# A ring of three pairs of PSUM banks, divided by use

## The reference, cut to what matters

```python
x = x + _layernorm(_L0_ffn_ref(_layernorm(x), ...))
# _L0_ffn_ref: D = 128, H = 16 heads of 8, E = 8 experts, K = 2, FF = 512
q = (x @ Wq + bq); k = (x @ Wk + bk); v = (x @ Wv + bv)      # by head; q, k rotated
attn = softmax(einsum('bhqd,bhkd->bhqk', q, k) / sqrt(HD))   # 1024 x 1024 per head
x1 = layernorm(x + (attn @ v) @ Wo + bo)
# two best of eight experts per token, weighted
h = gelu(einsum('bsd,edf->bsef', x1, W1) + b1); y = einsum('bsef,efd->bsed', h, W2) + b2
return layernorm(x1 + sum_e comb_e * y_e)
```

## Time and profile before

| | |
|---|---|
| median of 2 runs | 2870.24 us (2866.96 to 2873.52) |
| the profiled execution | 2869.59 us, span 2867.9 us |
| VectorE busy | 2243.4 us, 78% |
| ScalarE busy | 1236.5 us, 43% |
| TensorE busy | 1195.6 us, 42% |
| GpSimd busy | 289.9 us, 10% |
| mean granted clock of TensorE | 0.94 |

### The profile page before, as it was taken

The page is one execution under the profiler, slowest core; times in us unless marked ns, Lnnn a source line. Parts: engine busy times, 40 slices in busy tenths (PEclk is TensorE's granted clock), DMA queues, the critical chain, the costliest instruction groups (busy, mean ns, idle before and its releaser), DMA issues. The chain is left out here.

```text
span 2867.9 us, 37860 instructions
## 1 busy us (share of the span) xinstructions
PE 1195.6 (42%) x7272; PEld 536.4 (19%) x7272; DVE 2243.4 (78%) x15187; ACT 1236.5 (43%) x3176; POOL 289.9 (10%) x425
## 2 busy tenths in 40 slices
PE   3010100101010000101004887788876887778697
PEld 1000000000000000000001111223421342133365
DVE  5999999999999999999975899856657665864133
ACT  1333333333333333333360556656655664567542
POOL 0000000000000000000010020031023212201211
PEclk9999999999999999999996899979987998889898
DMA  5000000000000000000034020103110212001100
GB/s 135 1 1 1 1 1 1 1 1 1 1 1 1 1 1 1 1 1 1 1 68 103 1 67 20 24 22 89 26 44 23 74 37 52 18 17 30 33 1 23
DMA packets 79603, 66.11 MB, mean 23 GB/s; under 512 B 8126, under 2 KB 64232, under 8 KB 79368
## 3 DMA queue, kind: packets, MB, share of 16 engines
q1 hardware_dynamic: 76296, 57.40, 8.3%
q0 software_dynamic: 3072, 6.30, 0.7%
HBM read 34.77 MB, written 28.57 MB: 22 GB/s over the span
## 5 line engine op out<-in xcount | busy, mean ns | idle before, releaser
L1309 DVE TENSOR_REDUCE nm_half<-pair 128x2 f32<-128x1024 f32 x512 | 611.7, 1219 | 224.1 <-PE pair L1557 188.6
L203 ACT ACTIVATE ex<-row,nmax 128x65 f32<-128x65 f32 x960 | 336.0, 350 | 923.8 <-DVE nmax L305 837.3
L1196 ACT ACTIVATE pt<-pair 128x1024 f32<-128x1024 f32 x512 | 510.2, 1027 | 389.2 <-PE pair L1567 357.9
L263 DVE SCALAR_TENSOR_TENSOR junk<-ex,tab 128x65 f32<-128x65 f32 x2850 | 620.0, 218 | 1.4 <-issue 0.4
L366 PE MATMUL p_s<-tab,bdg 128*128 128x32 f32 x120 | 31.9, 406 | 829.2 <-DVE tab L268 829.2
L1533 PE MATMUL p_o<-pt,va 128*9 128x512 f32 x2048 | 299.2, 659 | 9.7 <-ACT pt L1196 8.3
L268 DVE TENSOR_TENSOR tab<-raw,rz 128x1 f32<-128x1 f32 (+1 forms) x1890 | 284.8, 151 | 3.2 <-issue 1.1
L297 DVE SCALAR_TENSOR_TENSOR junk<-ex,rz,row 128x65 f32<-128x65 f32 x930 | 265.4, 285 | 3.0 <-issue 2.7
L1557 PE MATMUL pair<-ks,qs 48*128 48x512 bf16 x1024 | 212.8, 420 | 123.3 <-ACT pt L1196 75.4
L1567 PE MATMUL pair<-qs,ks 50*128 50x512 bf16 x1024 | 209.7, 414 | 62.4 <-DVE nm_half L1309 30.4
L263 DVE DVE_READ_ACCUMULATOR junk<-ex,tab 128x1 f32 x2850 | 233.8, 82 | 0.3
(11 more groups left out here) (254 smaller groups left out, 1908.1 us busy)
## 6 DMA issues: line engine op xcount, KB each, us to landing
parts_dram<-parts SPq DMA_DIRECT2D x48, 256.0 KB, 3.6
qs<-parts_dram SPq DMA_DIRECT2D x32, 192.0 KB, 4.8
ks<-parts_dram SPq DMA_DIRECT2D x32, 192.0 KB, 5.4
hid<-xs_dram SPq DMA_DIRECT2D x15, 256.0 KB, 2.9
ys_dram<-hid SPq DMA_DIRECT2D x15, 256.0 KB, 2.4
h_dram<-f SPq DMA_DIRECT2D x20, 128.0 KB, 2.5
x<-in_x SPq DMA_DIRECT2D x4, 512.0 KB, 8.4
w_W<-in_W SPq DMA_DIRECT2D x1, 2048.0 KB
```

The lines of the kernel that those rows point to most:

```text
L203: nc.scalar.activation(ex[:, r % 2, :], row[:, r % 2, 1:], ACT.Exp, bias=nmax[:, r % 2:r % 2 + 1], accum_out=z[:, r % 2:r % 2 + 1]).then_i ...
L263: nc.vector.scalar_tensor_tensor(junk[:, g, :], ex[:, k, :], 1.0, tab[:, g, r:r + ROW], ALU.mult, ALU.mult, accum_out=raw[:, g:g + 1]).the ...
L1196: nc.scalar.activation(pt[:, kt % 2, :, tokens(t)], pair[fill.pair][:, :, :], ACT.Exp, scale=SCALE).then_inc(s_exp, 1)
L1309: nc.vector.reduce_max(nm_half[:, t, hp % 2, :, q], pair[fill.pair][:, :, :], AX.X, negate=True)\
```

## The change

Two lists of uses take the place of one. Maxima (A) always use `pair[2]`, and an A waits for the maximum of the A before it. B, HS and HH alternate between `pair[0]` and `pair[1]`, and each waits for the evacuation of the use two before it of these three kinds. The list of steps, the tensors and the instructions are the same; only the pair and the value waited for differ.

```diff
--- before.py
+++ after.py
@@ -836,18 +836,20 @@
 
 
 
-    pairs = []
+    scores, maxima = [], []
 
     def one(steps, s, ring, n):
         for x in steps:
-            prior = pairs[-PAIRS] if len(pairs) >= PAIRS else None
-            fill = Fill(ring, n, len(pairs) % PAIRS, prior)
+            used = maxima if x[0] == "A" else scores
+            first, count = (2, 1) if x[0] == "A" else (0, 2)
+            prior = used[-count] if len(used) >= count else None
+            fill = Fill(ring, n, first + len(used) % count, prior)
             if x[0] == "T":
                 steps_of(x[1:], s - 1, fill)
             else:
                 steps_of(x, s, fill)
             if x[0] in ("A", "B", "HS", "HH"):
-                pairs.append((x[0], pair_index(x, s)))
+                used.append((x[0], pair_index(x, s)))
             n += bank_uses(x)
         return n
```

## The result

The changed kernel takes 3083.28 us (3080.42 to 3086.14, 2 runs) against 2870.24: a ratio of 1.0735, interval 1.0695 to 1.0775. It is slower, as forecast, but by 213 us where 131 were forecast, and 3 us beyond the range.

What follows compares the result with a forecast made beforehand. VectorE was taken to bound batch 0 (205 of 225 us), no engine being full in batches 1 to 3. Terms 12 + 81 + 38 = 131 us on 2870 gave 3000 us, 4.5% slower, range 2930 to 3080.

Steps and rivals of the forecast that it cites:

- Unit cost: Back-to-back maxima: with one pair, fill and evacuation alternate, 1.71 us apart instead of 1.13, or 1.93 at 1.2 GHz.
- the sum of 1.53: Between maxima at 2.4 GHz: A, PV, B and the next A start within 1.53 us, fitting into 1.71.
- Prologue, +12: Opening run of 16 maxima: 15 distances grow from 1.13 to 1.93 us, +12 us, hidden by nothing.
- Batch 0, +81: Batch 0: 160 maxima alternating with their fills, +68 us, plus some time at the lower clock, +13 us.
- I allow 8 of the 64 steps: Batch 0: 8 more loop steps at the lower clock, 1.67 us extra each, +13 us.
- my middle of 68: Batch 0: alternation alone costs +68 us, between +49 (other work and idle time absorbed) and +88 (neither absorbed).
- rival (a): Clock falls through batch 0: all 64 steps slow, 107 us in place of 13, 3094 us in all; chance 0.16.
- Batches 1 to 3, +38: Batches 1 to 3: +24 for eight stretches, +32 for bunched maxima, -18 for vanished exponential waits; between -20 and +75 us.
- the gain of 18 us from exponentials: Batches 1 to 3: a quarter of TensorE's 75.4 us idle before As on exponentials goes, -18 us.
- The 56 bunched ones: Batches 1 to 3: 56 maxima starting less than 1.3 us behind the one before lose 0.58 us each, +32 us.
- The eight stretches: Batches 1 to 3: eight stretches between expert groups, 11 maxima each, grow from 126.1 to 150.5 us, +24.
- Costed at nothing: Two pairs for exponentials and expert products, and the routed products' 21.5 us of idle time put down to maxima: 0 us.

Runs made afterwards that it cites:

- Filling the gaps: Changed kernel with matmuls whose result nobody reads added in batch 0, in 78 gaps between two maxima tiles holding at most one B: 3051.21 us, ratio 1.0599.
- the other order: Changed kernel with the second of two maxima tiles in batch 0 issued behind the value product PV, not directly behind the first: 3067.67 us, ratio 1.0672.
- the opposite division: Changed kernel with the split reversed, two pairs for maxima and one shared by exponentials and expert products: 2970.92 us, ratio 1.0348.

## Why the prediction was wrong

The direction and the alternation held; two terms of the sum failed: the time at the lower clock in batch 0, put far too low, and a gain in batches 1 to 3 that did not come.

*Unit cost.* 1.71 and 1.93 us: the prologue shows 1.93 to the hundredth. In batch 0 maxima with no other VectorE work between them start 1.71 to 1.73 us apart at 2.4 GHz, with PV and B in the gap as well, as the sum of 1.53 had it; at 1.2 GHz 1.93 is the usual distance with PV or B alone in the gap, and 2.79 with both. Right.

*Prologue, +12.* 12. Right.

*Batch 0, +81.* 119. The step that failed is "I allow 8 of the 64 steps" at the lower clock, +13. The clock was low for 205 of 345 us, 182 more than before, which is some 31 steps of 5.95 us. At the price I had worked out (1.67 us for such a step) that is 51 us, and 68 + 51 = 119; that it comes out to the us is luck. Filling the gaps took 152 us of low clock away and gave 36 us, which is a price of 0.24 for one us at the lower level where I had 0.28. By this estimate the clock costs some 43 us, at least, since the added matmuls are in the 36, and the alternation at most 76, within its bounds and a little above my middle of 68. I had the argument in hand, 0.66 busy against 0.80, and put it into rival (a) as all or nothing, 64 steps or 8; it came out half way, and I gave (a) 0.16.

The Trainium skill, "TensorE: Matmul & The Clock Gate", section "A second HAM failure mode: psum-queue depth-cycling", describes a kernel that cycles through PSUM banks, where small idle gaps make the clock swing between its levels. The trace agrees on the swing, with 18 spells at the lower level in batch 0; that the gaps cause it is not shown here, as the other order left one of them empty and the clock as it was.

*Batches 1 to 3, +38.* 86, or 83 with the change in them alone (68 in its profiled execution, at the clock of before). The second step that failed is the gain of 18 us from exponentials. It was judged by one stall, in which the maximum happened to be early. In these batches TensorE waited 73 us for exponentials before As; now it waits 134 us for maxima, and exponentials are no longer among the main releasers there. The distances between maxima, sorted as the prediction had them, say the same. The 56 bunched ones lost 34 us in the changed kernel and 31 in the run with the change in these batches alone, against +32: right. The eight stretches lost 30 and 22, against +24. The other 199, which the gain should have made 18 us shorter, became 19 and 11 us longer. Why they did is open; part of the 19 goes with the clock, which lay low for 80 us more than before and only 7 more in the other run. The +24 rested on a misreading: the bounds of the earlier trace rows cut maxima at both ends, so a distance there was 1.52 us (80 of them in 121.6), not 1.43, and at 1.71 they would have lost 15. That 30 came out goes with the lower clock: in the changed kernel three of the eight had it for about two thirds of their time and took 2.10 or 2.11 us a distance, the three at 2.4 GHz throughout 1.72 or 1.73.

*Costed at nothing.* The two pairs for exponentials and products cost nothing that shows: what follows batch 3 took 1 us more, and the product's idle time rose from 30.4 to 36.6 us only, mostly its own issue. Right; the opposite division shows that one pair would have cost.

*The range.* The ends of the terms gave 3058, and half of (a), 47 us, on top of them would have been 3105; the range stopped at 3080, which did not allow for the clock and the missing gain at once.

## What to carry to other kernels

A shared ring gives each kind of use the slack of the others; count, for each kind, how often it directly follows itself, before a buffer is taken from it. With one buffer the distance is evacuation + release + fill + start, and what the filling engine has to do after the fill comes on top as far as it is longer than the evacuation. When a change adds idle time to TensorE, price the stage at both clock levels and let the range reach from one to the other, rather than make the lower level a rival of its own; here it came out in between. And when a wait goes, look for the wait that ends next at the same place, over all its cases and not at one: 73 us of waits for exponentials went, and 134 us of waits for maxima came.

## What the hardware showed unexpectedly

The mean granted clock of an execution says little here. In the first layer, where TensorE is a tenth busy or so, the profile records it at 0.99 before the change and at 0.50 after, from 60 to 1540 us, yet the second layer starts at 1549 and 1547 us, and the matmuls of line 350 last 461 ns on average in both. Only by stage, and beside the duration of the same instruction (a PV of 1.05 or 1.89 us), can the clock be read.

A clock of 0.70 came with two different orders of the same work (345 and 332 us), 0.91 with idle matmuls added to it (309 us, TensorE busy for 33 us longer).
